# Attention queries and keys as two float32r words in half-array row tiles, instead of three bf16 words over the full array

## The chip, the cores and the metric

The kernel runs on one core of a Trainium2 chip. The metric is the device time of one execution in microseconds (us). Engines are named as in the profile: PE is TensorE, DVE is VectorE, ACT is ScalarE, POOL is GpSimd, SP is the engine that issues most DMAs.

## The reference

The input x has 4 sequences of 2048 positions and 256 features. The result adds an attention branch and an FFN branch to x, both fed with a layer norm of x.

```python
xn = layernorm(x)
q, k, v = xn @ Wq.T, xn @ Wk.T, xn @ Wv.T        # 16 heads of 16
q, k = rope(q), rope(k)
scores = einsum('bhqd,bhkd->bhqk', q, k) / 4      # causal
attn = softmax(scores)
a = einsum('bhqk,bhkd->bhqd', attn, v) @ Wo.T
g, y = fp4(xn) @ fp4(w_gate).T, fp4(xn) @ fp4(w_up).T   # 704 inner features
f = fp4(silu(g) * y) @ fp4(w_down).T
out = x + a + f
```

Wq and Wk are scaled up about sevenfold, so scores are large and their small parts matter. fp4 quantises and dequantises in blocks of 16.

## The kernel before, in words

There are three stages, each a block with a barrier at its end.

**Stage 1** (`norm_ffn_qkv`, L123) goes over 16 groups of 512 positions. Each group is normed, put through the FFN and projected. Queries and keys get rope on DVE (`rope_products` L700, `rope_sums` L710) in the f32 tile `raw`, 4 x 512 columns. Then they are split in three bf16 words. ACT casts the first (L517), DVE subtracts (`second_rest`, L720), ACT casts the second (L534), DVE subtracts again into the third (`third_part`, L725). SP stores each word with four DMAs to the DRAM tensor `qkp` (`store_part`, L291). Each engine's order in a group is written out by hand: `group` at L479 for ACT, at L775 for DVE, `jobs` at L229 for PE. DVE's order runs scale (L100), round (L109, L111, L115), the additions to x (L748), with `second_rest` at L792 and `third_part` at L802.

**Stage 2** (`attention`, L951) has 16 iterations: 4 head groups of 4 heads times 4 sequences. SP loads the words stacked along the rows (`stack`, L1032), once per pair of word products that counts: six products of 16 rows, 96 rows of bf16, in three DMAs per stack. Three more rows of the keys hold ones and three of the queries the words of the row's negated maximum (99 rows). One iteration interleaves two kinds of work.
- Maximum tiles (`max_tile`, L1142): PE computes scores with the queries stationary (L1153, 96 rows), DVE reduces them to a maximum per row (L1322; on the diagonal L1327 with the mask added). Four PSUM slots. About half of them are for the next iteration. The maxima go through DVE (L1339), POOL (L1285 to L1291), PE (L1164), DVE (L1344) and four small DMAs (L1068) into rows 96 to 98 of the queries.
- Score steps: there are 40 per iteration, one for each pair of a query block of 512 and a key block of 128 at or below the diagonal, with four heads each. PE computes the transposed scores (L1178, 99 rows, up to 512 columns) in one of three PSUM slots. In a diagonal step it adds the causal mask to 128 columns of the same bank by a matmul of 128 rows (L1183). ACT takes the exponential (L1247). PE weights the values (`weigh`, L1198) for two steps at a time, four heads in four column tiles of 32 columns in f32. A query block qb has 4 x qb full steps and 4 diagonal ones, of 512, 384, 256 and 128 columns. After each block ACT copies the sums (L1254) and SP stores them.

The order of PE's work in an iteration is the string ORDER (L55): s is a score (a pair of weightings comes ahead of every eighth one, `attention_plan` L815), t a maximum tile, r the transposition of the maxima, o a store. PE, ACT and DVE all walk the plan in that order. Heads of a score go 0, 1, 2, 3.

**Stage 3** (`out_projection`, L1372) divides by the sums of the exponentials (a spread by PE, L1442, of 48 rows; a product, L1477), projects (L1450) and adds x (L1487).

## Time and profile before

| | |
|---|---|
| median of 3 runs | 2567.84 us (2566.38 to 2568.65) |
| span of the profiled execution | 2561.9 us (a total of its own beside the span is not given) |
| PE busy | 2440.4 us, 95% |
| DVE busy | 2236.7 us, 87% |
| ACT busy | 1594.3 us, 62% |
| exponentials, L1247 | 2560, 1158.6 us |
| maximum tiles' reductions, L1322 and L1327 | 956.8 us and 469.5 us |
| scores, L1178, and maximum matmuls, L1153 | 2560 each, 812.6 us and 778.0 us |
| granted PE clock, mean | 0.979 |

The busy time of a group adds the durations of its instructions once where they overlap. A matmul's duration has its run through the array in it, so the durations of successive matmuls overlap by about 0.17 us; the distance between their starts is what each one costs. f32 matmuls leave two records each.

### The profile page before, as it was taken

To read this page: it belongs to the slowest core of one execution; us is meant where nothing else is said; L and a number is where in the kernel's file an instruction comes from. 1 tells how busy PE (TensorE), PEld (TensorE's weight loads), DVE (VectorE), ACT (ScalarE), POOL (GpSimd) and SP (SyncE) were. 2 spreads that over 40 slices of the span, in tenths; PEclk is the share of its full clock that TensorE was granted. 3 is DMA by queue.
4 is the path that set the end of the run, shared out by engine and by line. 5 is a ranking of instruction groups with operands and counts; after the bars stand their busy time and mean duration, and the time that the engine had idled before them with its cause. 6 is when DMAs were issued, how large, how long until landed. Compare 5 with 4: busy or idle time off the path is not lost. (4 is left out here: it accounts for less than half of the span.)

```text
span 2561.9 us, 51480 instructions
## 1 busy us (share of the span) xinstructions
PE 2440.4 (95%) x14338; PEld 1170.2 (46%) x14338; DVE 2236.7 (87%) x4841; ACT 1594.3 (62%) x3260; POOL 166.3 (6%) x466
## 2 busy tenths in 40 slices
PE   5999999999996999999999999999999999999987
PEld 3555555555564234434444344344344344443335
DVE  8999999999996989898899899889888888998834
ACT  3545554554552277777777777777777777777740
POOL 2001101101101000000000000000000000000010
PEclk8999999999998699999999999999999999999999
DMA  6212112122123412212112122122122121120034
GB/s 199 74 56 67 64 64 69 56 70 71 54 72 90 113 35 61 70 33 67 43 54 73 31 62 67 35 62 74 35 61 69 33 68 41 55 61 6 20 125 173
DMA packets 141411, 168.57 MB, mean 66 GB/s; under 512 B 14048, under 2 KB 107536, under 8 KB 141200
## 3 DMA queue, kind: packets, MB, share of 16 engines
q1 hardware_dynamic: 137856, 159.49, 19.9%
q10 hardware_dynamic: 3344, 6.41, 0.7%
q8 instruction: 115, 1.88, 0.3%
q14 instruction: 96, 0.79, 0.1%
HBM read 97.17 MB, written 67.90 MB: 64 GB/s over the span
## 5 line engine op out<-in xcount | busy, mean ns | idle before, releaser
L1247 ACT ACTIVATE prob<-score 128x512 f32<-128x512 f32 (+3 forms) x2560 | 1158.6, 542 | 390.2 <-PE score L1178 192.1
L1322 DVE TENSOR_REDUCE top<-tile 128x1 f32<-128x512 f32 x1536 | 956.8, 680 | 104.0 <-PE tile L1153 95.7
L1178 PE MATMUL score<-qs,ks 99*128 99x512 bf16 (+3 forms) x2560 | 812.6, 350 | 7.8 <-ACT prob L1247 3.1
L1153 PE MATMUL tile<-ks,qs 96*128 96x512 bf16 (+3 forms) x2560 | 778.0, 355 | 25.7 <-DMA ks<-qkp 16.5
L1198 PE MATMUL acc<-prob,vs 128*32 128x512 f32 (+3 forms) x5120 | 535.3, 536 | 0.0
L1327 DVE CUSTOM_DVE_ANT_0 tile<-tile,mask 128x128 f32<-128x128 f32 (+3 forms) x1024 | 469.5, 518 | 61.5 <-PE tile L1153 59.3
L1178 PEld LDWEIGHTS score<-qs,ks 99*128 99x128 bf16 x2560 | 244.6, 97 | 414.5 <-ACT prob L1247 225.6
L1153 PEld LDWEIGHTS tile<-ks,qs 96*128 96x128 bf16 x2560 | 239.0, 98 | 298.0 <-DVE top L1322 84.6
L349 PE MATMUL gu<-wguT,xT 128*128 128x512 f32 (+1 forms) x768 | 310.7, 557 | 0.0
L1198 PEld LDWEIGHTS acc<-prob,vs 128*32 128x32 f32 x5120 | 133.9, 109 | 244.1 <-issue 138.9
L1183 PE MATMUL score<-identb,maskb 128*128 128x128 bf16 x1024 | 212.2, 220 | 0.0
L349 PEld LDWEIGHTS gu<-wguT,xT 128*128 128x128 f32 x768 | 143.6, 190 | 144.9 <-issue 122.8
L393 PE MATMUL misc<-wdT,hT 128*128 128x256 f32 x768 | 178.9, 383 | 1.3 <-ACT hT L472 1.3
L393 PEld LDWEIGHTS misc<-wdT,hT 128*128 128x128 f32 x768 | 143.8, 190 | 31.4 <-issue 11.3
L1327 DVE DVE_READ_ACCUMULATOR2_ANT top<- 128x1 f32 x1024 | 140.2, 137 | 0.0
L375 PE MATMUL misc<-xT,wqkvT_sb 128*128 128x512 f32 x256 | 118.4, 606 | 7.5 <-ACT xT L472 7.5
L1183 PEld LDWEIGHTS score<-identb,maskb 128*128 128x128 bf16 x1024 | 100.8, 98 | 38.7 <-issue 0.7
L1285 POOL CAST top_parts<-topm 128x16 bf16<-128x16 f32 x64 | 16.3, 254 | 1495.6 <-DVE topm L1339 1495.6
L492 ACT ACTIVATE silu<-gu 128x704 f32<-128x704 f32 x64 | 48.2, 753 | 90.0 <-PE gu L349 90.0
L109 DVE SCALAR_TENSOR_TENSOR scaled<-magic,scaled 128x704 f32<-128x704 f32 (+1 forms) x96 | 78.6, 818 | 19.2 <-ACT magic L477 19.2
L472 ACT COPY hT<-misc 128x512 f32<-128x512 f32 (+1 forms) x128 | 58.0, 482 | 58.1 <-PE misc L389 57.4
L477 ACT ACTIVATE magic<-scaled 128x704 f32<-128x704 f32 (+1 forms) x96 | 70.9, 738 | 30.4 <-DVE scaled L100 30.3
(130 smaller groups left out, 1723.0 us busy)
## 6 DMA issues: line engine op xcount, KB each, us to landing
qkp<-parts SPq DMA_DIRECT2D x192, 128.0 KB
vscr<-vt SPq DMA_DIRECT2D x16, 1024.0 KB, 5.4
vs<-vscr SPq DMA_DIRECT2D x16, 1024.0 KB, 6.1
oscr<-acc_sb SPq DMA_DIRECT2D x64, 256.0 KB, 2.1
qs<-qkp SPq DMA_DIRECT2D x64, 192.0 KB, 3.4
ks<-qkp SPq DMA_DIRECT2D x64, 192.0 KB, 3.3
x_all<-in_x SPq DMA_DIRECT2D x16, 512.0 KB, 9.0
qs<-qkp SPq DMA_DIRECT2D x64, 128.0 KB, 3.1
```

The lines of the kernel that those rows point to most:

```text
L109: link(nc.vector.scalar_tensor_tensor(out=scaled, in0=magic, scalar=1.25 * MAGIC, in1=scaled, op0=ALU.max, op1=ALU.add))
L349: mm = nc.tensor.matmul(gu[:, t % 2, c0:c0 + w], xT[:, KT + k, t * P:(t + 1) * P], wguT[:, k, c0:c0 + w], start=(k == 0), stop=(k == KT - 1))
L375: mm = nc.tensor.matmul(bank, wqkvT[:, k, t * P:(t + 1) * P], xT[:, k, :], start=(k == 0), stop=(k == KT - 1))
L393: mm = nc.tensor.matmul(bank[:, 0:DIM], hT[:, t % 2, i, :], wdT[:, i, :], start=(i == 0), stop=(i == IT - 1))
L477: nc.scalar.activation(magic[:, par, 0:w], scaled[:, par, 0:w], ACT.Abs, scale=MAGIC).then_inc(magic_ready, 1)
L1153: mm = nc.tensor.matmul(bank[:, h * width:(h + 1) * width], qs[par][0:ROWS, h0 + h, q0:q0 + P], ks[par][0:ROWS, h0 + h, k0:k0 + width], st ...
L1178: mm = nc.tensor.matmul(bank[:, 0:width], ks[par][0:ROWS_M, h, kb * P:(kb + 1) * P], qs[par][0:ROWS_M, h, qb * GROUP + off:(qb + 1) * GROU ...
L1183: mm = nc.tensor.matmul(bank[:, 0:P], maskb[:], identb[:], start=False, stop=True, skip_group_check=True)
L1198: mm = nc.tensor.matmul(acc[h * VW:(h + 1) * VW, off:GROUP], vs[par][:, kb // GT, kb % GT, h, :], prob[:, (HG * n + h) % PROB_SLOTS, 0:GRO ...
L1247: nc.scalar.activation(prob[:, k % PROB_SLOTS, 0:width], score[:, k % SCORE_SLOTS, 0:width], ACT.Exp, scale=HEAD ** -0.5).then_inc(probs_r ...
L1322: nc.vector.tensor_reduce(top[:, j, h0, c:c + 1], bank, AX.X, ALU.max).then_inc(tile_taken, 1)
L1327: last = nc.vector.tensor_tensor_reduce(out=head, in0=head, in1=mask[:, GROUP - width:GROUP], scale=1.0, scalar=MASK, op0=ALU.add, op1=ALU ...
```

## The change

- Queries and keys after rope are split in two f32 words. DVE takes the first with a bitwise AND that clears the low 12 bits (`high_part`, after the first `scale_h`), and the second by one subtraction (`low_part`, where `second_rest` stood). ACT's two casts go, and so does DVE's `third_part`. SP stores two words (8 DMAs of f32) instead of three (12 of bf16).
- A stack is three products of 16 rows, 48 rows of f32, and 51 with the maximum and the ones. Heads 0 and 2 lie in rows 0 to 63, heads 1 and 3 in rows 64 to 127; a stack is loaded with four DMAs. Scores and maximum matmuls read them as float32r. The mask, the transposed maxima and the weighting of the values are unchanged.
- The smallest diagonal maximum tiles hold two heads instead of four, and tiles of two heads hold heads of one side. This makes four tiles more an iteration, and ORDER has 4 letters t more.
- The ones are set by DVE (first buffers) and POOL (second); SP waits for them ahead of the first load of keys.

```diff
-ROWS = TERMS * HEAD
+SPLITS = 2
+HIGH_BITS = -(1 << 12)
+ROWS = SPLITS * (SPLITS + 1) // 2 * HEAD
 ROWS_M = ROWS + PARTS
+SIDE = 64
+SIDES = P // SIDE
+LOADS = SPLITS * SIDES
...
                 magnitude_h(1)
-                act.wait_ge(rope_ready, g + 2)
-                act.wait_ge(parts_stored, g * (PARTS * 4 * 16) + 1)
-                nc.scalar.copy(parts[:, 0, :, :], raw[:]).then_inc(part1_ready, 1)
                 gate(3)
...
                 taken("qk", 1, ahead=1)
-                act.wait_ge(rest_ready, g + 2)
-                nc.scalar.copy(parts[:, 1, :, :], turned[:]).then_inc(part2_ready, 1)
                 taken("qk", 2, ahead=1)
...
-            def second_rest(g):
+            def high_part(g):
+
+                dve.wait_ge(rope_ready, g + 2)
+                dve.wait_ge(parts_stored, g * (SPLITS * 4 * 16) + 1)
+                nc.vector.tensor_scalar(parts[:, 0, :, :].bitcast(I32), raw[:].bitcast(I32), HIGH_BITS, None,
+                                        ALU.bitwise_and).then_inc(part1_ready, 1)
+
+            def low_part(g):
 
                 dve.wait_ge(part1_ready, g + 1)
-                nc.vector.tensor_tensor(turned[:], raw[:], parts[:, 0, :, :], ALU.subtract).then_inc(rest_ready, 1)
-
-            def third_part(g):
-
-                dve.wait_ge(part2_ready, g + 1)
-                nc.vector.tensor_tensor(parts[:, 2, :, :], turned[:], parts[:, 1, :, :],
-                                        ALU.subtract).then_inc(part3_ready, 1)
+                nc.vector.tensor_tensor(parts[:, 1, :, :], raw[:], parts[:, 0, :, :],
+                                        ALU.subtract).then_inc(raw_free, 1)
...
                 scale_h(g, 0)
+                high_part(g)
                 round_h(g, more, 0)
...
-            heads = (4, 2, 1, 1)[j]
-            for h in range(0, HG, heads):
+            heads = (2, 2, 1, 1)[j]
+            for h in range(HG // heads):
                 tiles.append(("tile", n, qb, j, qb, h, heads, (j + 1) * P))
...
-                for parts in range(PARTS, 0, -1):
-                    first = (PARTS - parts) * HEAD if which else 0
-                    sp.dma_start(buf[row:row + parts * HEAD, :, c * GROUP:(c + 1) * GROUP],
-                                 src[first:first + parts * HEAD]).then_inc(loaded, 16)
+                for parts in range(SPLITS, 0, -1):
+                    first = (SPLITS - parts) * HEAD if which else 0
+                    for side in range(SIDES):
+                        sp.dma_start(buf[side * SIDE + row:side * SIDE + row + parts * HEAD, :, c * GROUP:(c + 1) * GROUP],
+                                     src[first:first + parts * HEAD, side::SIDES, :]).then_inc(loaded, 16)
...
                 stack(qs[it], 0, it, c, q_loaded[it][c])
+                if c == 0:
+                    sp.wait_ge(ones_ready[it], SIDES)
                 stack(ks[it], 1, it, c, k_loaded[it][c])
...
+            def stacked(buf, h, rows, first, width):
+
+                side = h % SIDES * SIDE
+                return buf[side:side + rows, h // SIDES, first:first + width].bitcast(F32R)
...
                     mm = nc.tensor.matmul(bank[:, h * width:(h + 1) * width],
-                                          qs[par][0:ROWS, h0 + h, q0:q0 + P], ks[par][0:ROWS, h0 + h, k0:k0 + width],
+                                          stacked(qs[par], h0 + h * SIDES, ROWS, q0, P),
+                                          stacked(ks[par], h0 + h * SIDES, ROWS, k0, width),
                                           start=(h == 0), stop=True, skip_group_check=True)
...
-                mm = nc.tensor.matmul(bank[:, 0:width], ks[par][0:ROWS_M, h, kb * P:(kb + 1) * P],
-                                      qs[par][0:ROWS_M, h, qb * GROUP + off:(qb + 1) * GROUP],
-                                      start=True, stop=True)
+                mm = nc.tensor.matmul(bank[:, 0:width], stacked(ks[par], h, ROWS_M, kb * P, P),
+                                      stacked(qs[par], h, ROWS_M, qb * GROUP + off, width), start=True, stop=True)
                 if j is not None:
 
                     mm = nc.tensor.matmul(bank[:, 0:P], maskb[:], identb[:], start=False, stop=True,
                                           skip_group_check=True)
...
+            for side in range(0, P, SIDE):
+                nc.vector.memset(ks[0][side + SIDE // 2:side + SIDE, :, :].rearrange("p h c -> p (h c)"), 1.0
+                                 ).then_inc(ones_ready[0], 1)
```

## Rows read from the trace of the kernel before

**Rows 1.** Windows: start:end, length; busy us (count) of PE, PEld, DVE, ACT, POOL; clock, DMA.

```profile
400.00:448.59 48.59, 45.69 (x170) 28.51 (x169) 44.93 (x62) 24.78 (x41) 5.13 (x14) 1.00 0.19 65
875.00:1273.00 398.00, 396.94 (x2802) 163.05 (x2801) 356.35 (x926) 297.77 (x651) 16.11 (x64) 0.99 0.17 50
```

**Rows 2.** Timeline of ACT: start us, us, engine, line; the copies after each query block.

```profile
976.71 0.59 ACT L1254 COPY acc_sb<-acc 128x512 f32<-128x512 f32 x1 [0.70 <-PE acc L1198]
...
1006.05 0.59 ACT L1254 COPY acc_sb<-acc 128x512 f32<-128x512 f32 x1
1035.75 0.59 ACT L1254 COPY acc_sb<-acc 128x512 f32<-128x512 f32 x1
1075.99 0.59 ACT L1254 COPY acc_sb<-acc 128x512 f32<-128x512 f32 x1 [0.71 <-PE acc L1198]
```

**Rows 3.** Timeline of ACT: exponentials of full steps, in brackets the wait before.

```profile
1041.51 4.03 ACT L1247 ACTIVATE prob<-score 128x512 f32<-128x512 f32 x8 [1.23 <-PE score L1178]
...
1068.99 3.10 ACT L1247 ACTIVATE prob<-score 128x512 f32<-128x512 f32 x8 [1.31 <-PE score L1183]
...
2440.22 4.03 ACT L1247 ACTIVATE prob<-score 128x512 f32<-128x512 f32 x8 [1.19 <-PE score L1178]
```

**Rows 4.** Windows: the first query block of an iteration, four diagonal steps.

```profile
976.71:986.25 9.54, 9.54 (x83) 4.74 (x82) 9.38 (x21) 7.93 (x21) 1.00 (x4) 1.00 0.70 223
```

**Rows 5.** Timeline of PE: mask, scores and weighting in attention.

```profile
1203.24 0.22 PE L1183 MATMUL score<-identb,maskb 128*128 128x128 bf16 x1
1203.30 0.38 PE L1178 MATMUL score<-qs,ks 99*128 99x512 bf16 x1
...
1204.17 0.38 PE L1178 MATMUL score<-qs,ks 99*128 99x512 bf16 x1
1204.48 0.86 PE L1198 MATMUL acc<-prob,vs 128*32 128x256 f32 x16
1205.27 0.39 PE L1178 MATMUL score<-qs,ks 99*128 99x512 bf16 x1
```

**Rows 6.** Timeline of PE: the spread and the projection in stage 3.

```profile
2512.51 0.60 PE L1442 MATMUL o_spread<-last_recips,pickb 48*128 48x512 bf16 x2
2513.04 3.72 PE L1450 MATMUL o_prod<-woT_sb,scaledT 128*128 128x256 f32 x16
2516.70 0.60 PE L1442 MATMUL o_spread<-last_recips,pickb 48*128 48x512 bf16 x2
```

**Rows 7.** Timeline of PE: f32 matmuls of the FFN, 1408 columns twice.

```profile
404.57 4.89 PE L349 MATMUL gu<-wguT,xT 128*128 128x512 f32 x12
409.30 1.03 PE L379 MATMUL misc<-wqkvT_sb,xT 128*128 128x256 f32 x4
```

**Rows 8.** Groups by line and form: count, busy us, mean ns, idle before.

```profile
L1178 PEld LDWEIGHTS score<-qs,ks 99*128 99x128 bf16 x2560 | 244.6, 97 | 414.5 <-ACT prob L1247 225.6 <-issue 83.7
L1153 PEld LDWEIGHTS tile<-ks,qs 96*128 96x128 bf16 x2560 | 239.0, 98 | 298.0 <-DVE top L1322 84.6 <-DVE top L1327 76.3 <-issue 20.8
L1183 PE MATMUL score<-identb,maskb 128*128 128x128 bf16 x1024 | 212.2, 220 | 0.0
```

**Rows 9.** Timeline of DVE: the same rounding in two successive groups of stage 1.

```profile
400.24 0.89 DVE L109 SCALAR_TENSOR_TENSOR scaled<-magic,scaled 128x704 f32<-128x704 f32 x1 [1.27 <-ACT magic L477]
...
448.59 0.89 DVE L109 SCALAR_TENSOR_TENSOR scaled<-magic,scaled 128x704 f32<-128x704 f32 x1 [1.27 <-ACT magic L477]
```

**Rows 10.** Groups by line and form: subtractions and casts of the splitting.

```profile
L720 DVE TENSOR_TENSOR turned<-raw,parts 128x2048 f32<-128x2048 f32 x16 | 36.5, 2284 | 0.0
L725 DVE TENSOR_TENSOR parts<-turned,parts 128x2048 bf16<-128x2048 f32 x16 | 36.5, 2283 | 0.0
L534 ACT CAST parts<-turned 128x2048 bf16<-128x2048 f32 x16 | 30.4, 1902 | 1.4 <-DVE turned L720 1.4
L517 ACT CAST parts<-raw 128x2048 bf16<-128x2048 f32 x16 | 30.2, 1887 | 0.0
```

**Rows 11.** Timeline across the seam of stages 1 and 2.

```profile
812.57 0.42 DVE L748 TENSOR_TENSOR x_all<-misc,x_all 128x256 f32<-128x256 f32 x1 [2.04 <-PE misc L393]
821.72 2.03 SPq L1040 DMA_DIRECT2D qs<-qkp  x3
...
822.68 6.96 POOL L1273 MEMSET ks<- 32x4096 f32 x2 [88.02 <-issue]
```

More of the change, by code:

```diff
@@ L24 @@
 BF16 = mybir.dt.bfloat16
+F32R = mybir.dt.float32r
 AX = mybir.AxisListType
@@ L453, in take @@
                     if t == 0:
[L455 removed]
+                        act.wait_ge(raw_free, group + 1)
                     dst, src = raw[:, t, :], bank
@@ L948, in split_recips, with attention @@
     return nc.gpsimd.tensor_tensor(parts[2], rest, parts[1], ALU.subtract)
-def attention(nc, d, identf, qs0, ks0, ahead, sums, pickb, recips):
+def attention(nc, d, identf, qs0, ks0, ahead, pickb, recips):
     plan, STEPS = attention_plan()
@@ L991, in attention @@
         top_parts = sb("top_parts", [P, QB, P], BF16)
-        row = sb("row", [ROW_COLS, QB, P], BF16)
+        row = sb("row", [ROW_COLS, QB, P])
         acc_sb = sb("acc_sb", [P, 2, GROUP])
@@ L1271, in _ @@
                 pool.sem_inc(s, n)
-            for par in range(2):
-                nc.gpsimd.memset(ks[par][ROWS:P, :, :].rearrange("p h c -> p (h c)").bitcast(F32), ONE_PAIR
-                                 ).then_inc(ones_ready, 1)
-            pool.wait_ge(ones_ready, 2)
+            for side in range(0, P, SIDE):
+                nc.gpsimd.memset(ks[1][side + SIDE // 2:side + SIDE, :, :].rearrange("p h c -> p (h c)"), 1.0
+                                 ).then_inc(ones_ready[1], 1)
+            pool.wait_ge(ones_ready[1], SIDES)
             TOP_LINKS = 3
@@ L1309, in _ @@
         def _(dve):
+            for side in range(0, P, SIDE):
+                nc.vector.memset(ks[0][side + SIDE // 2:side + SIDE, :, :].rearrange("p h c -> p (h c)"), 1.0
+                                 ).then_inc(ones_ready[0], 1)
             nc.vector.memset(top_parts[:, :, ROW_COLS:P], 0.0).then_inc(identb_ready, 1)
```

60 lines of the change are left out of this document (26 added, 34 removed).

## The prediction

> **What bounds the kernel now.** I read the profile from the outside in. The windows of equal stretches [rows 1] show two stages. Up to about 813 us (norm, FFN, projections) PE and DVE are both over 90% busy. In the 16 iterations of attention that follow (first window from 875 us) PE is busy 99.7% of the time, DVE 90%, ACT 75%. So attention looks TensorE-bound, and a change that lets two heads' scores share the array looks like a gain. Two further views cut this down.
>
> The copies of the finished accumulator [rows 2] mark the steps. One iteration takes 1075.99 - 976.71 = 99.3 us (the starts of two copies one iteration apart). A query block of 12 full and 4 diagonal steps takes 40.2 us, one of 8 full and 4 diagonal 29.7 us, so a full step costs (40.2 - 29.7) / 4 = 2.6 us. An iteration is then 24 full steps, about 63 us, and 16 diagonal steps, about 36 us.
>
> The exponentials [rows 3] show what a pair of full steps needs at least. Eight exponentials start every 5.2 to 5.7 us in an ordinary iteration (27.5 us for five such pairs, 5.50 each). In the last iteration, where the maxima are done, they still take 5.22 us: 4.03 us of ACT and 1.19 us of waiting for a score behind the weighting of the values. Score slots and the weighting set this, not the tiles. A full pair can therefore lose at most about 0.3 us to a faster PE. The diagonal steps are where PE's work sets the time; but in the first of them (976.71 to 986.25 us) DVE is busy 9.38 of 9.54 us too [rows 4].
>
> **What PE does at a change of form.** Starts of matmuls give their true pitch (durations overlap). A mask of 128 columns is followed by the next score after 0.06 us, which is its streaming (128 columns at 2.4 GHz are 0.053): bf16 and the full array on both sides, nothing lost [rows 5]. The weighting uses column tiles of 32 and f32. It starts at 1204.48, 0.31 us after a score whose 512 columns stream in 0.21, so 0.10 us are lost going in. Its 16 records last 0.79 us to the next start; their streaming is 4 x (256 + 128) columns at 2.4 GHz, 0.64 us, so 0.14 us are lost coming out. A round trip costs 0.24 us. In the output projection two 48-row bf16 matmuls stand between 128-row f32 ones [rows 6]: 0.53 us for 2 x 0.213 of streaming, and 3.66 us for 16 x 256 columns at two cycles (3.45 us with the small gap per record): 0.10 + 0.21 = 0.31 us. Among f32 matmuls of one form nothing is lost: 12 records that need 4.69 us take 4.73 [rows 7]. These rows do not tell whether the loss is from the data type or from the part of the array that is used; both differ each time.
>
> **Part 1, the mask.** After the change a score is 51 rows of float32r in a half of the array; the mask stays a 128-row bf16 matmul onto the same bank. So each of the 64 masks of an iteration (1024 / 16, [rows 8]) now stands between two changes of form. At 0.24 us, from the same stage, this is 64 x 0.24 = 15.4 us an iteration; at 0.31 it is 19.8; at nothing, if float32r and bf16 rows of either height follow freely, 0. I take 15.4. It lies on PE's path in the diagonal steps.
>
> The Trainium skill (TensorEngine Tiling (Array Packing), Key Properties) says that changing the tiling mode, not just the tile, drains the engine, and gives no figure. By that rule the mask pays, by a reading of the rows as a change of type alone it pays as well; the trace agrees that something is paid and cannot say for which.
>
> **Part 2, the pairs.** 160 scores and 160 maximum matmuls an iteration [rows 8] now take 48 or 51 rows, head by head in alternating halves. Walking the new ORDER and pairing neighbours of different halves gives 121 pairs: 88 in full steps, 33 in diagonal ones (a mask follows each score there, so only a maximum matmul with its neighbour pairs). If a pair costs its longer member, the 33 save 4.8 us (sum of the shorter widths, 0.053 us per 128 columns). The 88 would free 16.7 us of PE, but full pairs have at most 12 x 0.29 = 3.5 us to give; I take half, 1.7. That different parts of the array run together is seen only for column tiles: 16 weighting records in 0.79 us, a quarter of their serial time [rows 5]. For row tiles the bounds are 0 and 8.3 us; I take 6.5.
>
> The skill (TensorE: Matmul & The Clock Gate, Part 3) reports 3.07x, not 4x, for four row tiles. As an estimate from that page, pairs worth about three quarters would make the iteration some 1.5 us longer than I sum it.
>
> **Part 3, float32r's price.** No row shows it. A bf16 record streams one column per cycle; each of the two records of an f32 matmul takes two (0.43 us for 512, [rows 7]). Two records of two passes look like the products of two words of 12 bits on each side; float32r with words of 12 bits would be one of the four. I take one cycle, bound it by two, and price two as a rival.
>
> Iteration: +15.4 - 6.5 = +8.9 us; times 16, **+142 us**.
>
> **Part 4, the FFN stage.** A group takes 448.59 - 400.24 = 48.35 us between equal instructions of DVE [rows 9]. DVE loses two subtractions of 2.28 us each [rows 10] and gains one like them plus a bitwise AND over the same 2048 columns, which no row shows: bounded by nothing and by 2.28 us, and I take the upper end, the nearest row's. The AND stands where DVE now waits 1.27 us for ACT's magnitude, so at most 1.0 us of it is on the path: 1.3 to 2.3 us saved a group. PE's own idle time in such a group is 48.59 - 45.69 = 2.9 us [rows 1], so PE follows. ACT loses two casts of 1.9 us [rows 10]; ACT is busy half the group, so they were beside other work and I count nothing. The AND now waits on DVE's queue for the last stores; these are issued 20 us before and cover it. I take 1.3 x 15 = **-20 us** (0 to -35).
>
> Queues: eight stores a group of 256 KB replace twelve of 128; a stack of queries or keys is four issues instead of three, of 2.03 / 3 = 0.68 us each [rows 11], so 8 x 0.68 = 5 us more of SP's queue an iteration, for loads that are made an iteration ahead; hidden. The row's four copies double in size, 3 to 6 KB, small. If the cover went, a wait would be a few us once a block. At the seam, the third part's stores no longer trail DVE's last work (the new stage starts at 821.7, DVE's last addition ended at 812.99), up to -8 us; but the first key load now waits for two memsets by DVE, 3.5 us each by POOL's row (7.0 us for two), up to +6. I take 0 [rows 11]. DVE's four extra tiles an iteration cost only a handshake.
>
> **Sum.** +142 - 20 = +122 us. The page's span is 2561.9 us, the median of the runs 2567.84, so some 6 us lie outside the span and stay. 2568 + 122 = **2690 us**. Its own range: price 0.15 and all 8.3 saved, FFN -35: 2555; price 0.31, pairs 4.8, FFN 0: 2808. I say 2590 to 2800.
>
> **Rivals.**
> - The switch is free (faster). Place: the masks. Then diagonal steps save what DVE's load [rows 4] allows of 4.8, say half, and full ones 1.7: about 4 an iteration, -64 - 20 = 2484 us. For it: no loss between 99 and 128 rows in bf16 [rows 5]. Against: the 0.31 us of [rows 6]. The sign turns at a round trip of (6.5 + 20/16) / 64 = 0.12 us.
> - The halves don't overlap: +15.4 to 19.8 an iteration, no savings: 2794 to 2865 us. For it: no row tiles in the trace.
> - float32r takes two cycles a column: 19.0 us more of streaming in the diagonal steps, 9.6 back from pairs, and 39 - 33.5 in the full ones: with the masks' 15.4 that is +30 an iteration, about 3030 us. For it: f32's two cycles a record.
> - Price and savings cancel, a round trip of about 0.12 us: 2568.
>
> **Chances.** Forecast 0.47, free switch 0.30, no overlap 0.08, two cycles 0.11, cancel 0.04. The range 2470 to 2850 leaves out two cycles and the ends. The likeliest case's range stands above. Faster 0.31 (the free switch and the forecast's edge), same 0.04, slower 0.65; 0.2% is 5 us, about what a measurement can tell here.
>
> **What would show it.** In the timeline of PE: mask to next score start 0.2 us or more, and score to mask 0.09 over streaming, confirms part 1; 0.06 and 0.00 refutes it. Two neighbours starting a few ns apart confirms the pairs. The query block of four diagonal steps should grow from 9.5 us [rows 4] to about 12, full pairs stay at 5.2 to 5.5. FFN groups should take 46 to 47 us. I am wrong if the iteration falls under 99 us.

## The result and the profile after: slower by 32%

The changed kernel takes 3395.61 us (median of 4 runs, 3386.46 to 3407.26), the kernel before on the same chip 2567.11 us (4 runs, 2564.69 to 2568.65). The ratio is 1.3228, 95% interval 1.3197 to 1.326. The forecast was 2690, its range ended at 2850: the sign was right, the size was not.

The page of the changed kernel, engines and slices (the clock is in tenths of full speed):

```profile
span 3397.4 us, 51717 instructions
...
PE 3280.6 (97%) x14338; PEld 1568.2 (46%) x14338; DVE 2268.9 (67%) x4843; ACT 1610.4 (47%) x3228; POOL 172.4 (5%) x466
...
PEclk8999999997666677668666676767677666767669
...
L1253 ACT ACTIVATE prob<-score 128x512 f32<-128x512 f32 (+3 forms) x2560 | 1226.4, 542 | 1127.8 <-PE score L1190 677.9
L1331 DVE TENSOR_REDUCE top<-tile 128x1 f32<-128x512 f32 x1536 | 977.2, 685 | 707.8 <-PE tile L1160 696.9
```

The first nine slices, the feed-forward stage, are as full as before. Then the clock line drops from nines to sixes and sevens, while PE stays 97% busy. ACT and DVE do nearly the work they did before (1610 and 2269 us busy, 1594 and 2237 before) and wait for PE: 1128 us ahead of the exponentials, 678 of it behind the mask (L1190), and 708 us ahead of the reductions. Windows of attention say the same (columns as in [rows 1]):

```profile
900.00:2300.00 1400.00, 1387.39 (x6501) 595.27 (x6504) 845.31 (x2125) 725.85 (x1508) 36.18 (x144) 0.69 0.11 36
...
1285.00:1290.00 5.00, 4.79 (x34) 1.93 (x32) 4.26 (x14) 3.92 (x8) 0.00 (x0) 1.00 0.24 61
1305.00:1330.00 25.00, 25.00 (x99) 10.43 (x102) 11.87 (x27) 8.84 (x21) 1.01 (x4) 0.50 0.28 85
```

The granted clock is 0.69 of 2.4 GHz on average, where [rows 1] had 0.99. It is a mixture of two levels: in the full steps at 1285 us it is 2.4 GHz, and from 1305 to 1330 us, the end of one iteration's diagonals and the start of the next, 1.2 GHz with PE busy all the time.

The copies of the accumulator, three iterations apart (timeline of ACT), to be set beside [rows 2]:

```profile
1016.25 0.58 ACT L1260 COPY acc_sb<-acc 128x512 f32<-128x512 f32 x1 [1.91 <-PE acc L1205]
...
1473.42 0.58 ACT L1260 COPY acc_sb<-acc 128x512 f32<-128x512 f32 x1 [1.91 <-PE acc L1205]
```

(1473.42 - 1016.25) / 3 = 152.4 us an iteration, 53.1 more than 99.3. Sixteen iterations make +849 us; less 10 by the time that attention begins (below) that is +839, and +829 was measured. So the whole loss is in attention.

PE's timeline inside a stretch at full clock, and one at half clock:

```profile
1302.64 0.49 PE L1160 MATMUL tile<-ks,qs 48*128 48x512 f32 x1
1302.64 0.44 PE L1186 MATMUL score<-qs,ks 51*128 51x384 f32 x1
...
1303.23 0.43 PE L1186 MATMUL score<-qs,ks 51*128 51x384 f32 x1
1303.59 0.23 PE L1190 MATMUL score<-identb,maskb 128*128 128x128 bf16 x1
1303.75 0.50 PE L1160 MATMUL tile<-ks,qs 48*128 48x512 f32 x2
...
1311.15 0.47 PE L1186 MATMUL score<-qs,ks 51*128 51x128 f32 x1
1311.55 0.29 PE L1190 MATMUL score<-identb,maskb 128*128 128x128 bf16 x1
1311.77 0.47 PE L1186 MATMUL score<-qs,ks 51*128 51x128 f32 x1
```

Two things the forecast asked for are there. Neighbours of different halves start together (1302.64 twice): the pairs exist. And the mask costs more than its streaming: the lone score of 384 columns at 1303.23 streams in 0.16 us, yet the mask starts 0.36 us later, and the next matmul 0.16 us after the mask's start where 128 columns stream in 0.053. That is 0.20 + 0.11 = 0.31 us a round trip. At half clock it is 0.40 - 0.107 = 0.29 and 0.22 - 0.107 = 0.11, together 0.40 us.

The feed-forward stage (timeline of DVE; L715 is the new AND, one group apart):

```profile
391.05 1.23 DVE L715 TENSOR_SCALAR parts<-raw 128x2048 int32<-128x2048 int32 x1
...
438.36 1.22 DVE L715 TENSOR_SCALAR parts<-raw 128x2048 int32<-128x2048 int32 x1
```

A group takes 438.36 - 391.05 = 47.3 us against 48.35 [rows 9], so 1.04 less. Where `third_part` stood, the next rounding (L113, at 424.13 us) now waits 1.03 us for ACT's magnitude (L477).

The seam, after (timeline of all engines) and then the first maximum of the kernel before (timeline of DVE):

```profile
806.28 3.47 DVE L1317 MEMSET ks<- 32x4096 f32 x1 [5.81 <-PEq L130]
...
814.16 2.47 SPq L1039 DMA_DIRECT2D ks<-qkp  x4
...
819.45 0.30 DVE L1336 CUSTOM_DVE_ANT_0 tile<-tile,mask 128x128 f32<-128x128 f32 x1 [5.03 <-issue]
```

```profile
829.79 0.30 DVE L1327 CUSTOM_DVE_ANT_0 tile<-tile,mask 128x128 f32<-128x128 f32 x1 [7.77 <-PE tile L1153]
```

DVE's last addition of the groups starts at 800.04 us, 12.5 earlier than in [rows 11]. The first maximum comes only 10.3 us earlier: the new stage begins sooner after that addition (its first memset at 806.28 us), but the two memsets of the ones then hold the first key load until 814.16.

### The profile page after: what moved, and what is told of

Same layout as the page of the kernel before. It is cut to its first block and busy times, and to the rows that moved or that the text cites. A ratio compares the mean times of both kernels' runs of the same rounds, so it can differ in the third digit from the quotient of the medians.

```text
span 3397.4 us, 51717 instructions
## 1 busy us (share of the span) xinstructions
PE 3280.6 (97%) x14338; PEld 1568.2 (46%) x14338; DVE 2268.9 (67%) x4843; ACT 1610.4 (47%) x3228; POOL 172.4 (5%) x466
## 5 line engine op out<-in xcount | busy, mean ns | idle before, releaser
L1253 ACT ACTIVATE prob<-score 128x512 f32<-128x512 f32 (+3 forms) x2560 | 1226.4, 542 | 1127.8 <-PE score L1190 677.9
L1331 DVE TENSOR_REDUCE top<-tile 128x1 f32<-128x512 f32 x1536 | 977.2, 685 | 707.8 <-PE tile L1160 696.9
L1186 PE MATMUL score<-qs,ks 51*128 51x512 f32 (+3 forms) x2560 | 1153.3, 523 | 21.7 <-ACT prob L1253 20.2
L1160 PE MATMUL tile<-ks,qs 48*128 48x512 f32 (+3 forms) x2560 | 975.9, 523 | 21.8 <-DMA ks<-qkp 18.6
L1205 PE MATMUL acc<-prob,vs 128*32 128x512 f32 (+3 forms) x5120 | 865.1, 818 | 0.0
L1186 PEld LDWEIGHTS score<-qs,ks 51*128 51x128 f32 x2560 | 552.2, 233 | 486.0 <-issue 244.4
L1160 PEld LDWEIGHTS tile<-ks,qs 48*128 48x128 f32 x2560 | 453.1, 233 | 231.0 <-issue 85.8
L1205 PEld LDWEIGHTS acc<-prob,vs 128*32 128x32 f32 x5120 | 177.3, 146 | 407.0 <-issue 219.3
L1190 PE MATMUL score<-identb,maskb 128*128 128x128 bf16 x1024 | 269.2, 263 | 0.0
L1190 PEld LDWEIGHTS score<-identb,maskb 128*128 128x128 bf16 x1024 | 103.4, 101 | 315.0 <-issue 301.3
L113 DVE SCALAR_TENSOR_TENSOR scaled<-magic,scaled 128x704 f32<-128x704 f32 (+1 forms) x96 | 78.5, 818 | 15.5 <-ACT magic L477 15.5
L115 DVE SCALAR_TENSOR_TENSOR scaled<-magic,scaled 128x704 f32<-128x704 f32 (+1 forms) x96 | 79.2, 825 | 3.3
```

Source lines behind the costliest of these rows:

```text
L113: link(nc.vector.scalar_tensor_tensor(out=scaled, in0=magic, scalar=1.25 * MAGIC, in1=scaled, op0=ALU.max, op1=ALU.add))
L115: link(nc.vector.scalar_tensor_tensor(out=scaled, in0=magic, scalar=1.25 * MAGIC, in1=scaled, op0=ALU.max, op1=ALU.subtract))
L1160: mm = nc.tensor.matmul(bank[:, h * width:(h + 1) * width], stacked(qs[par], h0 + h * SIDES, ROWS, q0, P), stacked(ks[par], h0 + h * SIDES ...
L1186: mm = nc.tensor.matmul(bank[:, 0:width], stacked(ks[par], h, ROWS_M, kb * P, P), stacked(qs[par], h, ROWS_M, qb * GROUP + off, width), st ...
L1190: mm = nc.tensor.matmul(bank[:, 0:P], maskb[:], identb[:], start=False, stop=True, skip_group_check=True)
L1205: mm = nc.tensor.matmul(acc[h * VW:(h + 1) * VW, off:GROUP], vs[par][:, kb // GT, kb % GT, h, :], prob[:, (HG * n + h) % PROB_SLOTS, 0:GRO ...
```

## The experiments

Three theories were on record at the start: **A**, the changes of form at the masks, which empty the array, take the clock down as well as their own time; **B**, matmuls that use only half of the rows take it down; **C**, float32r does. All need the granted clock beside the time. Each kernel was timed beside the kernel before on its own chip (2563 to 2568 us). The attention experiments were run once each, except the last (bf16 with 64 rows), which like the two of the feed-forward stage was run five times; repeated runs of one kernel here lie within 0.7% of each other. The windows shown are from 900 to 2300 us, columns as in [rows 1].

### The mask away

```diff
-                if j is not None:
-
-                    mm = nc.tensor.matmul(bank[:, 0:P], maskb[:], identb[:], start=False, stop=True,
-                                          skip_group_check=True)
...
-                                     ACT.Exp, scale=HEAD ** -0.5).then_inc(probs_ready, 1)
+                                     ACT.Exp, scale=0.001).then_inc(probs_ready, 1)
```

> The changed kernel without the 64 masks of an iteration; left out are the causal mask of the scores and the size of the exponent (its scale is 0.001, so that nothing overflows). In the changed kernel an iteration takes 154 us (before: 99.3) at a granted clock of about 0.68. Theory A (the array stands empty at each change between 64 rows and 128 rows, and that is also why the clock falls): without the masks the clock is back at 0.95 or more and an iteration takes 93 to 98 us, in all about 2470 to 2530 us. Theory B (half-height matmuls themselves make the clock fall): the clock stays between 0.6 and 0.8, an iteration takes 115 to 140 us, in all 2800 to 3150 us. Theory C (float32r as a type does it): as B.

Measured: 2825.97 us.

```profile
900.00:2300.00 1400.00, 1357.57 (x7733) 608.82 (x7730) 1073.46 (x2786) 892.73 (x1971) 48.19 (x192) 0.86 0.15 47
```

The 1024 masks and the form changes around them account for 570 us, 0.56 us each, nearly twice the 0.31 that one costs in the timeline. With them gone the clock rises from 0.69 to 0.86: more than B's 0.6 to 0.8, less than A's 0.95. So A names a part, and something remains that has nothing to do with the mask.

### The mask in the score's own half

The same mask, made of two bf16 matmuls of 64 rows and 64 columns in the half where the score's head lies, so that the shape in rows never changes at a mask.

```diff
-                    mm = nc.tensor.matmul(bank[:, 0:P], maskb[:], identb[:], start=False, stop=True,
-                                          skip_group_check=True)
+                    side = h % SIDES
+                    lo = side * SIDE
+                    for c in range(2):
+                        block_mask = maskb if c == side else maskb_swapped
+                        mm = nc.tensor.matmul(bank[:, c * SIDE:(c + 1) * SIDE], block_mask[lo:lo + SIDE, :],
+                                              identb[lo:lo + SIDE, lo:lo + SIDE], start=False, stop=True,
+                                              skip_group_check=True)
```

> The changed kernel with the mask as two bf16 matmuls of 64 rows and 64 columns each, in the same half of the array as the score, so that the tile form does not change at a mask and only the type does; the same mask is added. If the form is what costs (theory A): the score-to-mask and mask-to-score gaps of 0.20 and 0.10 us at full clock shrink to under 0.05 together, and the time is near that of the kernel without masks. If the change of type costs as much: the gaps stay, and the time stays above 3200 us. Theory B: gaps go, clock stays low, 2900 to 3200 us.

Measured: 2778.91 us, 617 us below the changed kernel, with all of its work done. Windows, and PE's timeline:

```profile
900.00:2300.00 1400.00, 1367.96 (x9502) 664.20 (x9494) 1099.75 (x2866) 913.41 (x2019) 50.55 (x200) 0.90 0.16 48
```

```profile
1328.14 0.20 PE L1196 MATMUL score<-identb,maskb 64*128 64x64 bf16 x1
1328.18 0.19 PE L1196 MATMUL score<-identb,maskb_swapped 64*128 64x64 bf16 x1
1328.21 0.48 PE L1163 MATMUL tile<-ks,qs 48*128 48x512 f32 x1
```

The granted clock is 1.00 in this stretch. Two masks of 64 columns start 0.04 us apart (their streaming is 0.027 each) and a float32r matmul follows 0.03 later. Float32r and bf16 stand side by side here and nothing is lost between them (the score ahead of them is some 0.1 us late, of which more below). So what is gone of the 0.31 us of the round trip was paid for the change in the rows, not for the data type. The clock is 0.90: still not 1.00. This kernel does more work on PE than the one without any mask, and yet is 47 us faster and has the higher clock (0.90 against 0.86). No run explains that difference.

### The form change alone, in the kernel before

```diff
-                    mm = nc.tensor.matmul(bank[:, 0:P], maskb[:], identb[:], start=False, stop=True,
+                    mm = nc.tensor.matmul(bank[:, 0:P], maskb[0:64, :], identb[0:64, :], start=False, stop=True,
```

> The kernel before with only the first 64 rows of the mask's matmul (left out: the mask of the other 64 columns): bf16 before and after, so that only the number of rows changes, 99 to 64 to 99, 64 times an iteration. If a change of the rows' form costs 0.24 to 0.31 us a round trip by itself, an iteration grows from 99.3 to 113 to 119 us, in all 2790 to 2890 us at full clock, more if the clock falls. If only a change of the type costs, it stays at 2567 us within 10 us.

Measured: 2751.31 us, 188 above the kernel before (2563.26). Windows, and PE's timeline:

```profile
900.00:2300.00 1400.00, 1397.73 (x8899) 510.25 (x8902) 1146.53 (x2927) 976.38 (x2065) 50.59 (x201) 1.00 0.16 48
```

```profile
1312.40 0.38 PE L1178 MATMUL score<-qs,ks 99*128 99x512 bf16 x1
1312.71 0.23 PE L1183 MATMUL score<-identb,maskb 64*128 64x128 bf16 x1
1312.87 0.39 PE L1178 MATMUL score<-qs,ks 99*128 99x512 bf16 x1
```

All bf16, and only the mask's rows changed from 128 to 64: 0.31 us from score to mask (0.213 streams) and 0.16 from mask to score (0.053), so 0.10 + 0.10 = 0.20 us a round trip. 64 of them are 12.8 us an iteration; 16 iterations make 205 us, and 188 came, below the expected range because the price is 0.20 and not 0.24 to 0.31. The clock stayed at 1.00: beside matmuls of 96 and 99 rows form changes do not lower it. Theory A, as a cause of its own for the clock, fell here.

### float32r over the whole array

Scores and maximum matmuls read all 128 rows as float32r (the rows that hold nothing are zero on the queries' side). The scores of two heads are then summed; the order of the work is that of the changed kernel.

```diff
-                return buf[side:side + rows, h // SIDES, first:first + width].bitcast(F32R)
+                return buf[:, h // SIDES, first:first + width].bitcast(F32R)
...
-                                     ACT.Exp, scale=HEAD ** -0.5).then_inc(probs_ready, 1)
+                                     ACT.Exp, scale=1e-7).then_inc(probs_ready, 1)
```

> The changed kernel with scores and maximum matmuls over all 128 rows of float32r, both heads of a column summed (left out: the separation of the heads, and the size of the exponent); rows that hold no words are zero. The form is then the full array throughout, no two heads overlap, and the type changes at each mask. Theory A: at most the type's gap at the masks, clock 0.95 or more, about 2550 to 2700 us. Theory B: as A. Theory C (float32r makes the clock fall, or takes two cycles a column): the clock stays at 0.6 to 0.8 or a 512-column score takes 0.43 us, over 2900 us.

Measured: 2714.8 us, **681 us faster** than the changed kernel, with twice the rows and no pairs, and 15 us above the upper end of what A and B expected. Windows, and the timelines of PE and of the weight loads:

```profile
900.00:2300.00 1400.00, 1399.02 (x9033) 802.74 (x9030) 1156.24 (x2968) 986.42 (x2093) 51.77 (x204) 1.00 0.16 49
```

```profile
1303.16 0.39 PE L1186 MATMUL score<-qs,ks 128*128 128x512 f32 x1
1303.38 0.23 PE L1190 MATMUL score<-identb,maskb 128*128 128x128 bf16 x1
1303.54 0.51 PE L1186 MATMUL score<-qs,ks 128*128 128x512 f32 x1
1303.89 0.23 PE L1190 MATMUL score<-identb,maskb 128*128 128x128 bf16 x1
```

```profile
1303.54 0.19 PEld L1186 LDWEIGHTS score<-qs,ks 128*128 128x128 f32 x1
```

Theory C fell as a cause of its own: the clock is 1.00 with float32r over all rows. (With few rows the type does matter for the clock; see the bf16 runs below.) Its streaming is one column a cycle (1303.16 to 1303.38 for 512 columns). What it does cost is the weights: 0.19 us for a load against 0.10 in bf16 [rows 8]. Around the short mask the next start is late (the mask at 1303.38 is followed after 0.16 us instead of 0.053, the score at 1303.54 after 0.35 instead of 0.213, so some 0.1 us lost at each); that it is the load that makes it late is inferred. From one copy to its like a whole iteration is 1315.20 - 1205.71 = 109.5 us, 10 more than before.

### Half the array and no overlap

The kernel with the mask in halves, all heads in rows 0 to 63 (the upper half is not used; heads 1 and 3 read the rows of 0 and 2).

```diff
-                side = h % SIDES * SIDE
+                side = 0
```

> The kernel with the mask in halves (2779 us, clock 0.91), with every score, maximum matmul and mask in rows 0 to 63 (left out: heads 1 and 3, whose scores are made from the words of heads 0 and 2). Nothing overlaps any more; only half of the array's rows are ever used for scores. If the clock follows how many rows work over time (theory B), it falls well below 0.91, to 0.5 to 0.8, and the time is 2900 to 3500 us. If it follows how much of the time PE streams (theory A: the gaps), PE now streams more of the time than with pairs, the clock is 0.95 or more, and the time is 2650 to 2780 us: 2779 less what the clock gave, plus the lost overlap.

Measured: 3549.16 us.

```profile
900.00:2300.00 1400.00, 1400.00 (x6594) 755.91 (x6594) 802.12 (x1993) 695.09 (x1403) 34.27 (x136) 0.65 0.11 33
```

```profile
1300.21 0.62 PE L1189 MATMUL score<-qs,ks 51*128 51x512 f32 x1
1300.64 0.62 PE L1163 MATMUL tile<-ks,qs 48*128 48x512 f32 x1
```

This is the clearest of all: PE is busy 1400.00 of 1400 us, there are no form changes at the masks, and the clock is 0.65. A busy record also covers a matmul's run through the array, so it could hide short gaps; the timeline of PE at a clock of 0.50 shows none here: 512 columns at 1.2 GHz are 0.427 us, and the next start comes after 0.43. An engine that never pauses is not thereby granted its full clock. Theory B forecast this in kind (0.5 to 0.8); the time came out 49 us above its range.

### All 64 rows of a half: with the 128-row mask, with the mask in halves

Both kernels read the rows from 48 or 51 up to the 64th too. They add nothing to the streaming.

```diff
-                return buf[side:side + rows, h // SIDES, first:first + width].bitcast(F32R)
+                return buf[side:side + SIDE, h // SIDES, first:first + width].bitcast(F32R)
```

> The changed kernel (masks of 128 rows, clock 0.68 in attention, 3396 us), with scores and maximum matmuls over all 64 rows of their half (left out: the size of the exponent; the maxima contain older ones). Theory: the clock follows how many rows of the array work over time, and the changes of form cost time by themselves and also thin out that work. Filling the halves then brings back most of the clock though the masks still change the form: 0.85 to 0.95 in attention, 2780 to 2950 us; what stays over the 2632 us of the same with masks in halves is the price of the changes at the full clock, at 0.20 to 0.30 us a mask 13 to 19 us an iteration, 205 to 310 us in all. Rival (the empty array at the changes is what the clock follows, rows only in second place): clock under 0.80, above 3050 us.

> The kernel with the mask in halves, with scores and maximum matmuls over all 64 rows of their half instead of 51 and 48; rows without words hold zeros and ones (left out: the size of the exponent; the maxima contain older ones). Streaming times are the same. If the clock counts rows that are switched on, 64 against 48 to 51, it rises from 0.91 to above 0.95 and the time falls to 2650 to 2740 us. If it depends on the half form, or on the data in it, it stays at 0.91 and 2779 within 30.

Measured: 3013.64 us and 2631.62 us. Windows of the first, then of the second:

```profile
900.00:2300.00 1400.00, 1377.13 (x7754) 624.00 (x7753) 1003.24 (x2546) 858.73 (x1797) 44.59 (x176) 0.88 0.14 43
```

```profile
900.00:2300.00 1400.00, 1362.92 (x10428) 704.66 (x10417) 1207.80 (x3143) 999.75 (x2214) 54.69 (x216) 0.99 0.18 52
```

The four kernels form a table, time and clock:

| | 48 and 51 rows | 64 rows |
|---|---|---|
| mask over 128 rows | 3396 us, 0.69 | 3014 us, 0.88 |
| mask in halves | 2779 us, 0.90 | 2632 us, 0.99 |

Thirteen to sixteen more rows, with nothing in them to compute, give 382 us back in one case and 147 in the other. The columns to stream are the same, and what differs in the windows is the clock. And a form change costs more when the clock is already falling: 617 us with 51 rows, 382 with 64. The first kernel met neither expectation: 3014 us lies between the 2780 to 2950 of the theory and the 3050 of its rival, with the clock (0.88) on the theory's side.

### Is it the data?

The kernels with 64 and 128 rows also carry another scale of the exponential. This run gives the scale alone to the kernel with the mask in halves.

```diff
-                                     ACT.Exp, scale=HEAD ** -0.5).then_inc(probs_ready, 1)
+                                     ACT.Exp, scale=1e-7).then_inc(probs_ready, 1)
```

> The kernel with the mask in two halves (48 and 51 rows), with one thing altered: the exponential's scale is 1e-7 instead of 1/4, so that the weights of the values come out near 1 and the output is not the attention's; it leaves no work out. The kernels with 64 rows, and the one with all 128, carry that scale too, so their higher clock could come from the data and not from the rows. Theory B (the rows at work set the clock): the data change nothing, the iteration stays at 109 us and the clock at 0.90: 2770 to 2790 us. Rival H (the data of the weighting set the clock): the clock rises to 0.97 or more and the iteration falls to 103 us, as with 64 rows: 2620 to 2660 us.

Measured: 2776.41 us.

```profile
900.00:2300.00 1400.00, 1368.03 (x9536) 667.90 (x9535) 1106.08 (x2880) 919.20 (x2030) 50.57 (x200) 0.90 0.16 48
```

Time and clock are those of the mask in halves. The rows, not the data of the weighting, made the difference in the table. What the added rows hold (zeros on one side, mostly ones on the other) was not varied.

### bf16 reads in the two halves

The kernel with the mask in halves reads only the upper 16 bits of each word, as bf16, with 48 and 51 rows and then with 64. The low bits of both words are left out.

```diff
-                return buf[side:side + rows, h // SIDES, first:first + width].bitcast(F32R)
+                return buf[side:side + rows, h // SIDES, first:first + width].bitcast(BF16)[:, 1::2]
```

> The kernel with the mask in halves, scores and maximum matmuls reading only the upper 16 bits of each word as bf16 (left out: the low bits of both words). Rows, halves, pairs and order stay; only the type differs. If half-height rows make the clock fall, it stays at 0.85 to 0.95 with bf16 too. If float32r is needed for it (theory C), the clock is above 0.97. The exposed weight load (a 512-column score takes 0.34 us to the next start where nothing hides it, against 0.21 of streaming) should go: weights of 98 instead of 190 ns. I expect 2600 to 2740 us; 2779 within 20 if the weight load is of no account.

> Masks in halves, all 64 rows, and bf16 (left out: the low 16 bits of each word, and the size of the exponent; the maxima contain older ones): the row-tile idea with its three costs taken away, no change of form at masks, no fallen clock, no f32 weights. If the three are all there is, PE is no longer the bound: an iteration takes 95 to 98 us instead of 99.3, the first stage and the seam give their 25 us, and the whole is 2490 to 2560 us, faster than the kernel before. If the order of the work and the three score slots hold PE back even so (full pairs of steps at 5.2 us or more), it is 2560 to 2600 us.

Measured: 2617.78 us, and with 64 rows 2578.53 us, ratio 1.0039 (1.0025 to 1.0053) to the kernel before. Windows of the first; windows (the last one is the last query block of the last iteration), then exponentials of full steps (timeline of ACT), of the second:

```profile
900.00:2300.00 1400.00, 1321.13 (x10438) 497.94 (x10436) 1210.06 (x3166) 1004.40 (x2225) 55.19 (x220) 0.96 0.18 53
```

```profile
900.00:2300.00 1400.00, 1315.53 (x10805) 507.21 (x10806) 1247.99 (x3248) 1034.40 (x2296) 56.56 (x224) 0.99 0.18 55
...
2437.99:2487.64 49.65, 43.57 (x220) 10.57 (x219) 2.96 (x1) 28.79 (x64) 9.10 (x4) 0.76 0.26 89
```

```profile
1240.49 4.03 ACT L1265 ACTIVATE prob<-score 128x512 f32<-128x512 f32 x8
1245.73 4.03 ACT L1265 ACTIVATE prob<-score 128x512 f32<-128x512 f32 x8 [1.21 <-PE score L1189]
1251.40 4.03 ACT L1265 ACTIVATE prob<-score 128x512 f32<-128x512 f32 x8 [1.64 <-PE score L1189]
```

The first run falls between its two expectations: with 48 and 51 rows in bf16 the clock is 0.96, not 0.90 and not 1.00. So the type has a part in the fall where rows are few, the rows have the rest, and no run tells by what the type acts. It also shows the 0.1 us that float32r cost ahead of a mask: a score of 384 columns (0.16 us of streaming) is followed by its mask after 0.18 us here (starts at 1301.58 and 1301.76 us), and after 0.28 in the same kernel with float32r (1327.86 and 1328.14), both at a clock of 1.00.

The second is the changed kernel with the faults taken out that the runs found: no form change at the masks, a clock of 0.99 from 900 to 2300 us, cheap weights. PE is now idle 6% of attention, and yet an iteration is as long as before: (1379.19 - 979.71) / 4 = 99.9 us between its copies, and (1475.12 - 976.71) / 5 = 99.7 in the kernel before. Eight exponentials start every 5.2 to 5.7 us, 1.2 to 1.6 us of each waiting for a score, as in [rows 3]. Two heads at once bring nothing in the full steps, because PE's streaming was not what held them.

Two things keep this run from being quite free of faults. In the last iteration, where there are no maximum tiles, its clock falls after all: the last query block runs at 0.76 and takes 49.65 us, where the kernel before takes 2472.63 - 2434.50 = 38.1 at 1.00, and eight exponentials start every 6.86 us (2459.09 and 2465.95) instead of 5.2. And the zeros of the added rows need two more memsets by DVE at the seam, so that the first maximum comes at 830.68 us, 11.2 later than in the changed kernel. Without these 11.5 and 11.2 us it would take some 2556 us, 0.5% less than the kernel before; that is an estimate from these rows, and no such kernel was run.

### The feed-forward stage: two attempts at its bound

First, in the kernel before, the first subtraction goes up into the wait of 1.27 us ahead of L109 [rows 9], where the changed kernel has its AND. The subtraction, like ACT's cast of the first word, reads that word as the upper half of the f32 value.

```diff
-                dve.wait_ge(part1_ready, g + 1)
-                nc.vector.tensor_tensor(turned[:], raw[:], parts[:, 0, :, :], ALU.subtract).then_inc(rest_ready, 1)
...
                 scale_h(g, 0)
+                second_rest(g)
                 round_h(g, more, 0)
...
                 scale_h(g, 3)
-                second_rest(g)
```

> The kernel before, with one thing that the changed one showed: DVE's first subtraction of the split stands where DVE waits for ACT's magnitude (1.27 us a group), which is possible because the first word is now cut off, not rounded (the upper 16 bits of each f32, read in place), so that the subtraction does not wait for ACT's copy. Nothing else changes; the three words still sum to the value. If the wait is filled as in the changed kernel (47.3 instead of 48.35 us a group), it saves 1.0 to 1.2 us in 16 groups: 2548 to 2553 us, ratio 0.993 to 0.996. If the subtraction of 2.28 us, longer than the wait, delays PE's next transposes by as much, nothing: 2564 to 2570 us.

Measured: 2588.82 us, ratio 1.0093 (1.0079 to 1.0107): 0.9% slower, outside both expectations (timeline of DVE).

```profile
405.81 2.29 DVE L720 TENSOR_TENSOR turned<-raw 128x2048 f32<-128x2048 f32 x1
...
430.50 0.42 DVE L748 TENSOR_TENSOR x_all<-misc,x_all 128x256 f32 x1 [3.79 <-PE misc L393]
```

The wait ahead of L109 is gone, and a longer one, 3.79 us for PE's down projection, stands where the subtraction stood; in the kernel before only 0.50 us was left there (L748, at 421.63 us). The subtraction had covered the rest. Filling one gap with work that covers another gains nothing.

Second, `third_part` goes to GpSimd (it follows the normalisation's statistics in that engine's loop).

```diff
+            def third_part(g):
+                await_on(pool, pool_passed, part2_ready, g + 1)
+                nc.gpsimd.tensor_tensor(parts[:, 2, :, :], turned[:], parts[:, 1, :, :],
+                                        ALU.subtract).then_inc(part3_ready, 1)
```

> The kernel before, with one operation of the feed-forward groups moved: the subtraction that makes the third bf16 word goes from VectorE to GpSimd, so that VectorE is spared 2.28 us in each of 16 groups, as in the changed kernel, where that subtraction is gone altogether. Theory F (the feed-forward group goes by VectorE, and by ScalarE's magnitude right behind it): in the changed kernel the group came down from 48.35 to 47.3 us, because the 2.28 us spared uncovered a wait of 1.03 us for ScalarE. Here the same wait is uncovered and nothing else is won, so 1.0 to 1.3 us of 16 groups: 2545 to 2556 us, ratio 0.991 to 0.996. Rival G: GpSimd's subtraction of 128 x 2048 takes so long that rope's products on VectorE wait for it, or it slows VectorE's own operations beside it: then the group is as long as before or longer, 2565 to 2600 us.

Measured: 2634.88 us, ratio 1.0267 (1.0253 to 1.0281). Timeline of POOL, then of DVE:

```profile
405.14 4.38 POOL L605 TENSOR_TENSOR parts<-turned,parts 128x2048 bf16<-128x2048 f32 x1 [30.24 <-ACT parts L534]
```

```profile
405.63 4.44 DVE L115 TENSOR_TENSOR xq<-scaled,nscale 128x512 f32<-128x512 f32 x1
...
415.01 0.69 DVE L115 TENSOR_TENSOR xq<-scaled,nscale 128x512 f32<-128x512 f32 x1
```

The rival held in kind, and the time is 35 us above its range. The product L115 that takes 0.69 us ten microseconds later takes 4.44 us beside GpSimd's subtraction, and ends 0.55 us after it. VectorE was spared 2.28 us and lost 3.75, and its waits for ScalarE grew from 1.3 to 3.5 us a group (2.0 ahead of L109, 1.2 ahead of L713, 0.3 ahead of L734). A group grew from 48.35 to 52.34 us (starts of L109 at 401.53 and 453.87), 16 x 4.0 = 64 of the 70 us.

## Why the prediction was right in sign and wrong in size

**The step that failed: every term of the sum was priced at the full granted clock.** "128 columns at 2.4 GHz are 0.053" was taken for the changed kernel too. [Rows 1] gives 0.99 and 1.00, but for matmuls of 96, 99 and 128 rows; nothing in the sum asked whether 48 and 51 rows keep it. The granted clock was 0.69.

How much of the 53.1 us an iteration is the clock's can only be bounded, since no kernel with this work ran at 1.00. If all of the 152.4 us went in step with the clock, an iteration would be 152.4 x 0.69 = 105 us at 1.00; some of it does not scale (the 0.40 against 0.31 of a round trip), so 105 is a lower end. The kernel with 64 rows and the mask in halves, at 0.99, takes (1396.17 - 983.87) / 4 = 103.1 us; with 64 round trips of 0.31 it would take 122.9, an upper end. By these estimates the clock has 30 to 47 us an iteration, 470 to 760 of the 829 us, and the direct costs are 6 to 24 us where the forecast had 8.9. Two kernels that stayed at 1.00 with one fault each lie 12.2 us (the form change in bf16, 111.5 us an iteration, copies at 1214.49 and 1325.94) and 10.2 us (float32r over the whole array, 109.5) above 99.3. If the two add up, the direct costs are near the upper end, and more than twice the forecast: the sum was too small even without the clock.

The sign was right by the forecast's own mechanism and not by luck, as far as the mask goes: a change of rows at the masks alone costs 188 us in the kernel before.

The trace of before gave no price for the clock, but it held a warning that the forecast did not use. In the first maximum tiles of attention, after PE had stood idle from 812.5 to 829 us, the clock is 0.50 (windows, and the timeline of PE, of the kernel before):

```profile
830.00:875.00 45.00, 40.49 (x87) 8.53 (x85) 44.86 (x135) 0.00 (x0) 2.00 (x8) 0.50 0.59 154
```

```profile
844.94 9.97 PE L1153 MATMUL tile<-ks,qs 96*128 96x512 bf16 x17 [0.16 <-DVE top L1327]
```

PE is busy 90% of this stretch by its records, with matmuls of 96 rows, and is held at 1.2 GHz for all of it. Here its starts leave gaps (10 us for 17 matmuls, 0.59 each, where 512 columns at 1.2 GHz are 0.427), because DVE, busy 44.86 of 45 us, sets the pace; at 885 us, with scores and weighting beside the maxima, it is 1.00. So 96 rows do not keep the full clock by themselves, and the number of rows is not the whole rule.

The Trainium skill (TensorE: Matmul & The Clock Gate, Part 1, "What's actually happening") says that the throttled state is the default and activity releases it. It ties the drop to idle time. By that the changed kernel, 97% busy, and the one-sided kernel, busy 1400.00 of 1400 us, would hold 2.4 GHz; they got 0.69 and 0.65. The measurements decide: that PE is busy in the profile does not tell the granted clock.

**Part 1, the mask: right in kind, its own price at the upper end.** 0.31 us a round trip at full clock, not 0.24, so 19.8 us an iteration and not 15.4. The runs also settle what the rows had left open: it is the rows that change (0.20 us in bf16 alone, and about nothing between float32r and bf16 in one half). The other 0.1 is of the size of the exposed float32r weight load. That splitting is inferred from separate kernels. The sentence of the Trainium skill (TensorEngine Tiling (Array Packing), Key Properties) that a change of tiling mode drains the engine fits these runs: time is lost at each change, 0.20 us for a round trip in bf16.

**Part 2, the pairs: right that they overlap, but the saving of 6.5 us was not seen.** They start together, and the full steps had almost nothing to give: with the clock restored and bf16 weights the pairs of full steps still take 5.2 to 5.7 us. Nor did the diagonal steps give their 4.8: in that kernel an iteration is 99.9 us against 99.7, and its first query block, with DVE busy 9.19 of 9.35 us (1180.27 to 1189.62), is 0.2 us shorter than [rows 4].

**Part 3, float32r: right for the streaming, but a term was missing.** One column a cycle. The weight load of 0.19 us was not in the sum. Between h_rows64 and h_bf16_64 (the pair of kernels with 64 rows) the data type is worth 53 us, 3.3 an iteration.

**Part 4, the feed-forward stage: right direction, a smaller sum.** 1.04 us a group came in the middle of the stage, not 1.3, and 12.5 us by its end for the 20 forecast. The AND takes 1.22 us, not 2.28, and so fits in the wait of 1.27; `third_part` gone uncovers 1.03 us of waiting for ACT. The Trainium skill (VectorE: DVE Perf Modes, "Mode 2×_2P") has single-source f32 operations run at two elements a cycle, which the trace bears out for this AND of 32-bit words, with 1.22 against 2.28 us; the row of a subtraction was the wrong neighbour for it.

**The seam: 0 forecast, +2 measured.** From the last addition to the first maximum it is 19.4 us after and 17.2 before: the stage starts sooner, the memsets take that back, as the two bounds (-8 and +6) had it.

**The rivals.** The free switch needed a round trip under 0.12 us; it is 0.31. The halves do overlap (the equal starts above). Two cycles a column did not happen. None of the rivals was the clock. That was the real omission: a mechanism whose cost multiplies every other term, with no chance given to it.

One check that the prediction names shows it at once: the query block of four diagonal steps was to grow from 9.5 us to about 12, and it takes 1336.20 - 1316.68 = 19.5 us.

```profile
1316.68 0.58 ACT L1260 COPY acc_sb<-acc 128x512 f32<-128x512 f32 x1 [1.91 <-PE acc L1205]
1336.20 0.59 ACT L1260 COPY acc_sb<-acc 128x512 f32<-128x512 f32 x1
```

No version that was run beats the kernel before.

## What to carry to other kernels

Before packing small matmuls into parts of the array, ask what the granted clock will be: a kernel may lose more by the clock of half-used rows than by the streaming it saves, and filling the rows up to the tile's height can be free. Look at the clock by stretches, in the trace of before too: a mean hides a stretch at half clock. Put a full-height matmul between half-height ones only where its round trip of 0.2 to 0.3 us is off the path. And look first at what the steps wait for; where the exponentials wait behind score slots and weighting, a faster TensorE gives nothing.

## What was not expected of the hardware

- The clock falls with TensorE busy all the time: 0.65 with 48 and 51 rows of float32r on one side, 0.90 where two halves overlap (0.96 in bf16), 0.99 with 64 rows, 1.00 with 99 or 128, from 900 to 2300 us. It is 0.76 with 64 rows in a last block without maximum tiles, and 0.50 with 96 rows in a stretch where TensorE starts a matmul every 0.59 us. Rows, type and the pace of the work all go with it; which quantity ties them together stays open.
- Form changes in the rows cost 0.20 us a round trip in bf16 at a clock of 1.00. The clock is lower with them only where the rows are few: 0.69 instead of 0.90 with 51 rows, 0.88 instead of 0.99 with 64, and 1.00 either way with 99.
- float32r streams a column a cycle and loads its weights in 0.19 us, bf16 in 0.10.
- A VectorE product of two SBUF operands beside a GpSimd subtraction went from 0.69 to 4.44 us: it seems to have been held until GpSimd was through.
